# An LSTM step whose wait for x's output gate columns is moved to the loop's beginning, and whose second new cell is computed ahead of the first half of h

## The reference, cut to what matters

```python
def attend(h):
    q = h @ Wq.T
    scores = einsum('bc,bsc->bs', q, context)
    alpha = softmax(scores)
    ctx = einsum('bs,bsc->bc', alpha, context)
    return tanh(concatenate([ctx, h]) @ Wout.T + b_out)

def step(carry, x_t):
    h, c, attn = carry
    gates = concatenate([x_t, attn]) @ W_ih.T + b_ih + h @ W_hh.T + b_hh
    i, f, g, o = split(gates, 4)
    c = sigmoid(f) * c + sigmoid(i) * tanh(g)
    h = sigmoid(o) * tanh(c)
    out = attend(h)
    return (h, c, out), out
```

## Time and profile before

| | us |
|---|---|
| median of 3 runs | 5704.32 (5700.22 to 5705.46) |
| the profiled execution | 5699.97 |
| its span | 5698.2 |
| from one step's scores to the next's | 7.26 |
| TensorE busy over the span | 5170.7 (91%) |
| VectorE busy over the span | 3385.5 (59%) |

### The profile page before, as it was taken

The page is one execution under the profiler, slowest core; times in us unless marked ns, Lnnn a source line. Parts: engine busy times, 40 slices in busy tenths (PEclk is TensorE's granted clock), DMA queues, the critical chain, the costliest instruction groups (busy, mean ns, idle before and its releaser), DMA issues. The chain is left out here.

```text
span 5698.2 us, 474379 instructions
## 1 busy us (share of the span) xinstructions
PE 5170.7 (91%) x214184; PEld 4093.5 (72%) x214184; DVE 3385.5 (59%) x15403; ACT 1942.1 (34%) x7968; POOL 340.9 (6%) x795
## 2 busy tenths in 40 slices
PE   9899999999999999999999999998688879796989
PEld 4788888888888888888888888887434334443433
DVE  5455555555555555555555555554798999999941
ACT  2244444344444443444444434442212222222221
POOL 0000000000000000000000000000111111111100
PEclk9999999999999999999999999999899889897999
DMA  2000000000000000000000000002111101010111
GB/s 97 38 2 2 2 2 2 2 2 2 2 2 2 2 2 2 2 2 2 2 2 2 2 2 2 2 2 76 56 52 39 41 17 56 26 58 23 51 39 57
DMA packets 60806, 111.58 MB, mean 20 GB/s; under 512 B 18308, under 2 KB 28452, under 8 KB 60204
## 3 DMA queue, kind: packets, MB, share of 16 engines
q1 hardware_dynamic: 59276, 109.42, 6.3%
q10 hardware_dynamic: 1440, 1.06, 0.1%
HBM read 99.92 MB, written 10.52 MB: 19 GB/s over the span
## 5 line engine op out<-in xcount | busy, mean ns | idle before, releaser
L868 PE MATMUL lstm_part_ps<-lstm_keys,lstm_hid 128*8 128x64 f32 x65536 | 1041.8, 219 | 200.2 <-DVE lstm_hid L1039 200.2
L868 PEld LDWEIGHTS lstm_part_ps<-lstm_keys,lstm_hid 128*8 128x8 f32 x65536 | 920.1, 90 | 342.3 <-DVE lstm_hid L1039 313.5
L891 PE MATMUL lstm_ctx_ps<-lstm_values,lstm_alpha 128*8 128x128 f32 (+1 forms) x49152 | 1029.1, 237 | 0.0
L891 PEld LDWEIGHTS lstm_ctx_ps<-lstm_values,lstm_alpha 128*8 128x8 f32 x49152 | 919.1, 90 | 23.5
L1061 DVE TENSOR_REDUCE lstm_neg_max<-lstm_part_ps 128x1 f32<-128x64 f32 x1024 | 230.0, 225 | 729.0 <-PE lstm_part_ps L868 729.0
L1021 DVE STREAM_TRANSPOSE lstm_gates<-lstm_half_ps 128x96 f32<-128x96 f32 x1026 | 290.2, 283 | 588.6 <-PE lstm_half_ps L826 564.3
L826 PE MATMUL lstm_half_ps<-lstm_w_hid,lstm_hid 128*25 128x96 f32 x16384 | 578.9, 248 | 1.2 <-issue 1.2
L1000 ACT ACTIVATE lstm_expo<-lstm_part_ps,lstm_neg_max 128x64 f32<-128x64 f32 x1024 | 320.8, 313 | 621.1 <-DVE lstm_neg_max L1061 621.1
L826 PE MATMUL lstm_half_ps<-lstm_w_attn,lstm_attn 128*25 128x96 f32 x16448 | 437.0, 246 | 0.0
L989 ACT ACTIVATE lstm_cell<-lstm_gates 128x12 f32<-128x12 f32 x1024 | 225.3, 220 | 431.1 <-DVE lstm_gates L1021 431.1
L2115 ACT ACTIVATE mix_gated<-mix_gate_ps 128x512 f32<-128x512 f32 (+1 forms) x192 | 107.8, 561 | 743.3 <-PE mix_gate_ps L1842 738.4
(11 more groups left out here) (333 smaller groups left out, 8485.7 us busy)
## 6 DMA issues: line engine op xcount, KB each, us to landing
mix_ring<-in_sm_chunks SPq DMA_DIRECT2D x112, 384.0 KB, 3.1
mix_ring<-in_mix_chunks SPq DMA_DIRECT2D x80, 384.0 KB, 3.1
lstm_xg<-xg_rows SPq DMA_DIRECT2D x514, 12.0 KB
lstm_xg<-xg_rows SPq DMA_DIRECT2D x513, 4.0 KB
xg_rows<-rec_lam SPq DMA_DIRECT2D x16, 512.0 KB, 2.6
xT<-in_xT SPq DMA_DIRECT2D x4, 512.0 KB, 9.3
ctxT<-in_ctxT SPq DMA_DIRECT2D x1, 2048.0 KB, 14.5
out_xT<-xT SPq DMA_DIRECT2D x4, 512.0 KB, 3.9
```

Of the source, the lines that this page charges most:

```text
L868: mm = pe.matmul(part_rows(score_ps[part], b), hid[:, k, lo:lo + SPACE], keys[:, k, b * SRC + c * SUB:b * SRC + (c + 1) * SUB], start=(n = ...
L891: mm = pe.matmul(part_rows(ctx_ps[n], b), alpha[:, b, c, SPACE - 1 - 2 * c:2 * SPACE - 1 - 2 * c], values[:, b * SC + c, ctx_cols[n]], sta ...
```

## The change

TensorE: the wait for `o_x_loaded` leaves `o_gate_x_hid` and stands at the beginning of the loop's iteration, ahead of the wait for the first half of h. The value waited for is the same, 16 (t + 2) at the beginning of iteration t, because the sums in question are those of `gates(t + 1)`. Ahead of the loop a wait for 16 takes its place for `gates(0)`. VectorE: `new_cell(t, 1)` stands ahead of `new_hidden(t, 0)`.

```diff
@@ o_gate_x_hid
-                    pe.wait_ge(o_x_loaded, 16 * (t + 1))
                     gate_sums(o_gate_ps, o_cols, place, xg[:, :], start=True).then_inc(o_x_used, 1)
@@ block.tensor
+                pe.wait_ge(o_x_loaded, 16)
                 gates(0)
                 next_x(0)
                 with pe.Fori(0, SEQ) as t:
+                    pe.wait_ge(o_x_loaded, 16 * (t + 2))
                     pe.wait_ge(h_ready[0], t + 1)
                     part_scores(0, 0)
@@ block.vector
                     cell_products(t, 1)
+                    new_cell(t, 1)
                     new_hidden(t, 0)
-                    new_cell(t, 1)
                     new_hidden(t, 1)
```

## The result

The changed kernel takes 5774.84 us (median of 4 runs, 5770.29 to 5785.58), against 5702.55 us for the kernel before in the same comparison. The ratio is 1.0129, with a 95% interval of 1.0112 to 1.0147: 72 us slower, where 5799 and a range of 5750 to 5852 had been forecast. The profiled execution took 5779.03 us; its span is 5777.2, 79.0 more than before.

A forecast was written before the change was run, and what follows sets the result against it. Bound taken: the step's loop through TensorE and h, 7.26 us. With the load's landing: 5.22 + 0.22 + 1.98 + 0.05 + 0.08 = 7.55, less 0.045 and 0.06, is 7.445; 95 us more gives 5799 us, range 5750 to 5852.

The forecast's parts named there:

- The bound and the new loop: Loop's beginning: the moved wait makes a step run from scores via x matmuls, load issue and landing to scores: 7.445 us.
- 5.115: TensorE, start of scores to end of x matmuls: 5.22 us before, less the 0.045 and 0.06 given back.
- 1.98 + 0.05 + 0.08: From load issue to scores: 1.98 us landing, 0.05 from semaphore to TensorE, 0.08 for the register instruction carrying the wait.
- The size: Whole loop: 7.445 us a step against 7.26, 0.185 more, 95 us in 512 steps.
- the 1.98 for the landing: 4 KB load of x: lands 1.98 us after issue, chosen between 1.56 and 2.14, near a 12 KB load's row.
- The wait that left the o gates: Behind `select(1)` in the o gates: x matmuls end 0.045 us a step sooner, 0.035 on the way through h.
- VectorE's exchange: First half of h 0.045 us later, 0.06 stall between halves' scores gone: gain 0.015 a step; behind a late load, 0.045 hidden.
- What the trace should show: Step about 7.44 us; scores' weight loads released by `lstm_xg` DMA; h's first half 0.2 us ahead; gap between halves gone.
- A: Rival: load lands in time, under 1.745 us after issue; step 7.21 us, gain of 26 us, 5678 us; chance 0.07.
- B: Rival: landing at 1.78 to 1.82 us, the two ways cancel, time within 11 us of 5704; chance 0.05.
- C: Rival: landing at the upper end, 2.14 us; 7.605 us a step, 177 us more, 5881 us; chance 0.08.
- The skill's rule: SyncE loads: skill gives about 0.6 us to first byte, making the change a gain; rows put first packet at 1.42.

The follow-up runs named there:

- the two delayed loads: A second, unread 4 KB load issued ahead of the o columns' load: in the changed kernel 6195.65 us (one execution), in the kernel before 5696.07 us, ratio 0.9997.
- the run with the landed wait: Kernel before with VectorE's exchange, plus a wait at the loop's beginning for the previous, already landed load: 5738.13 us, ratio 1.0072.

## Why the prediction was right, step by step

- **The bound and the new loop.** Right, and shown by the two delayed loads and by the wait alone. The measured step, taken apart: from the scores to the end of the x matmuls 5.10 us (5.115 forecast), 0.22 to the issue (0.22), and from the issue to the scores 2.05 in the step shown. On the average that last part is longer, what is left of 7.405 if the other two are the same in each step: 7.405 - 5.10 - 0.22 = 2.085, against 2.11 forecast (1.98 + 0.05 + 0.08).
- **The size.** 0.146 us a step instead of 0.185, 75 us instead of 95. Of the 0.04 between them 0.025 lies in the term for landing and reaction and 0.015 in the 5.115. No step of the argument failed; the sum was made of roundings that all went up. How the last part divides can be read from line 940: in the step shown 1.95 to the register instruction, where the landing and the semaphore had been put at 2.03, and about 0.1 from there to the matmul, where 0.08 had been put. So each term was near, but the 1.98 for the landing was a choice between 1.56 and 2.14, and no row fixed it there: below 1.745 the change would have been a gain of 26 us, at 2.14 a loss of 177 us. Its only support was the 12 KB load, which was read at a granted clock of 0.50, and the stretches of the step at 1.00. That it was so near is in part luck. (The range should read 5748 to 5850, 51 us to both sides of 5799; nothing hangs on it.)
- **The wait that left the o gates.** `select(1)` ends at 2006.94 and the x matmuls at 2007.07, 0.13 behind it instead of 0.18: the 0.05 is there. On the way through h, 0.035 a step had been counted; the wait ahead of h's part of the half gates gave 7.242 - 7.2125 = 0.030 over the exchange alone, of which it may have lost 0.01 again at its new place.
- **VectorE's exchange.** Right in all its terms: 0.046 and 0.061 for 0.045 and 0.06, and nothing in the changed kernel.
- **What the trace should show.** The first half of h stands 0.21 us ahead of the scores (0.2 forecast), and the gap between the halves is gone (the 128 matmuls take 1.97 instead of 2.04). One sign was wrong: the weight loads of the scores still name h as releaser, and only the matmuls name the DMA; why the profile names them differently, though both stand behind the same register instruction, no run shows. And the run with the landed wait shows that this name alone would have been no proof.
- **The rivals.** A needed the landing within 0.19 us of the last packet. After the change the register instruction with the wait starts 0.39 behind it (2008.85 to 2009.24), 1.95 after the issue, where A needed 1.745 + 0.05 at most and B, the near tie, 1.82 + 0.05; so both are out. C, 2.14 us to the landing, would have made a step of 7.6.
- **The skill's rule.** The first packet came 1.43 us after the start of the issue in the changed kernel, 1.42 before; counted from the end of the issue's instruction, which takes 0.65 and 0.64 us, it is 0.78 in both. The 0.6 us to the first byte for loads from SyncE that the Trainium skill gives ("DMA: Bandwidth & Descriptors", "Specifications") was seen in neither. The advice of the Trainium skill on the same page, in "Rules for kernel authors", to wait late, held against the loop's beginning: further down the step, ahead of h's part of the half gates, the same wait is met and costs 0.01 us a step or less. Latest of all was not best here: right at the use, in the o gates, it cost 0.03.

## What to carry to other kernels

A wait that is always met where it stands may not be met one step of the loop earlier: before moving it up, find the instruction that starts the transfer, add its time to land, and see whether that closes a new loop through the place. To take a met wait off a chain, move it, behind the landing, to work that ends in a pause anyway, and onto an instruction that has no other semaphore. And a releaser in the profile is a hint; what showed it here was to delay the suspected transfer and to see the step grow by as much.

## What the runs showed of the hardware

- A 4 KB load issued by SyncE took 1.4 us to its first packet, 1.95 us until the register instruction that waited for it started and 2.05 us until TensorE's matmul did, in the step shown; the average until the matmul, worked out from the steps' length, is 2.085. The 12 KB load ahead of the loop took 2.27.
- Where two waits of TensorE stood ahead of one matmul with no register instruction between them, one became an `EVENT_SEMAPHORE` of its own (51 ns). It stood where the pause ended, and the weight load started 0.06 us and the matmul 0.03 us later: 0.09 a step in two places, some 46 us in 512 steps, though the other semaphore had long been reached.
- The register instruction with its wait cost 0.03 us a step in the o gates, where no pause follows, and 0.01 or less in two places with a pause behind them (5.11 and 5.11 us against 5.10 without it).
